# The second layer's experts: engine loops instead of straight code, all shared blocks first

## The reference

```python
h = modulated(layernorm(x))                      # (4096, 128)
logits = h @ gate_w.T + gate_b                   # 8 experts
w, idx = softmax over the top 2 of the logits
def expert(h, w1, b1, w3, b3, w2, b2):           # w1, w3: (256, 128), w2: (128, 128)
    u = (h @ w1.T + b1) * (h @ w3.T + b3)        # (.., 256)
    g, l = min(u[..., ::2], 7), clip(u[..., 1::2], -7, 7)
    return (g * sigmoid(1.702 * g) * (l + 1)) @ w2.T + b2
y = sum over the two chosen e of w_e * expert_e(h)  +  shared_expert(h)
out = x + gate * y
```

## Time and profile before

| | us |
|---|---|
| median of 3 runs | 1839.58 (1836.76 to 1840.22) |
| profiled execution, its own time | 1833.77 |
| its span | 1832.0 |
| granted TensorE clock, mean | 0.877 |
| the mixture's blocks, from the first scatter | 1511 to 1832 |

### The profile page before, as it was taken

One profiled execution on the slowest core, in us unless ns is written; L12 is line 12 of the kernel. 1 busy time (PEld: TensorE's weight loads), 2 busy tenths in 40 slices (PEclk: granted clock), 3 DMA queues, 4 the chain that ended last, 5 costly groups with the idle time before them and its releaser, 6 DMA issues. The chain is left out here.

```text
span 1832.0 us, 41747 instructions
## 1 busy us (share of the span) xinstructions
PE 1461.2 (80%) x15040; PEld 996.7 (54%) x15040; DVE 1314.7 (72%) x3621; ACT 952.3 (52%) x2202; POOL 592.0 (32%) x584
## 2 busy tenths in 40 slices
PE   4277767776698569999999999999999577198490
PEld 2277667776643235555555555555555455187370
DVE  6899999997678736667666676666766685077286
ACT  7555555554311436666666666666666432066260
POOL 0876666770113334111111111111110107601415
PEclk7688888888699789999999999999999867599695
DMA  2400000000000012111111111111110001258352
GB/s 70 132 1 1 1 1 1 1 1 0 12 1 5 15 22 42 31 29 30 29 30 26 25 30 28 30 30 30 30 28 8 15 1 54 71 154 231 95 140 82
DMA packets 150357, 71.53 MB, mean 39 GB/s; under 512 B 95234, under 2 KB 135700, under 8 KB 150164
## 3 DMA queue, kind: packets, MB, share of 16 engines
q1 hardware_dynamic: 143316, 60.42, 15.1%
q0 software_dynamic: 4096, 8.40, 1.5%
q10 hardware_dynamic: 2752, 0.26, 0.1%
HBM read 38.11 MB, written 18.35 MB: 31 GB/s over the span
## 5 line engine op out<-in xcount | busy, mean ns | idle before, releaser
L1299 DVE TENSOR_REDUCE ntop<-score 128x1 f32<-128x512 f32 x512 | 317.9, 683 | 252.0 <-PE score L1178 252.0
L1256 ACT ACTIVATE prob<-score,ntop 128x512 f32<-128x512 f32 x512 | 317.5, 688 | 268.6 <-DVE ntop L1299 268.6
L440 ACT ACTIVATE hist<-zp 128x168 f32<-128x168 f32 (+1 forms) x768 | 224.4, 313 | 171.1 <-DVE zp L408 170.4
L1214 PE MATMUL turned<-ident,prob 128*128 128x128 f32 x2048 | 268.5, 280 | 1.8 <-DVE probT L1240 1.8
L490 PEld LDWEIGHTS py<-hist,diagC 128*128 128x128 f32 x2048 | 262.6, 214 | 0.0
L490 PE MATMUL py<-hist,diagC 128*128 128x128 f32 x2048 | 262.3, 296 | 0.0
L1178 PE MATMUL score<-ks,qs 64*128 64x512 f32 x1024 | 255.0, 616 | 0.0
L1214 PEld LDWEIGHTS turned<-ident,prob 128*128 128x128 f32 x2048 | 219.0, 141 | 49.1 <-issue 28.1
L460 POOL TENSOR_TENSOR xb<-xc,Bm 128x1024 f32<-128x1024 f32 x128 | 244.9, 1954 | 1.3
L403 DVE TENSOR_TENSOR gp<-hist,Ap 128x168 f32<-128x168 f32 (+1 forms) x768 | 229.7, 328 | 14.8 <-POOL xb L460 14.8
L408 DVE TENSOR_TENSOR zp<-gp,xb 128x168 f32<-128x168 f32 (+1 forms) x768 | 232.9, 333 | 0.0
(11 more groups left out here) (304 smaller groups left out, 1624.9 us busy)
## 6 DMA issues: line engine op xcount, KB each, us to landing
w<-in_ew SPq DMA_DIRECT2D x46, 320.0 KB
tb<-in_table SPq DMA_DIRECT2D x64, 127.1 KB
sorted_h<-nought SPq DMA_DIRECT2D x2, 2944.0 KB, 17.2
xs<-sorted_h SPq DMA_DIRECT2D x46, 128.0 KB
sorted_y<-ysb SPq DMA_DIRECT2D x46, 128.0 KB
ks<-k_sb SPq DMA_DIRECT2D x32, 128.0 KB
rel_q<-q_sb SPq DMA_DIRECT2D x248, 8.0 KB
key_q<-q_sb SPq DMA_DIRECT2D x248, 8.0 KB
```

The source lines that it names most:

```text
L440: nc.scalar.activation(hist[:, par, u, lo:hi], zp[j][:, 0:hi - lo], ACT.Tanh)\
L1214: last = nc.tensor.transpose(turned_ps[BANK[e]][:, j * P:(j + 1) * P], prob[G % 2][e][:, j * P:(j + 1) * P], ident[:, :])
L1256: nc.scalar.activation(prob[G % 2][e][:, :], score_ps[r][:, :], ACT.Exp, bias=ntop[:, G % 2, e:e + 1]).then_inc(prob_ready, 1)
L1299: v.tensor_reduce(ntop[:, G % 2, e:e + 1], score_ps[r][:, :], AX.X, ALU.max, negate=True)\
```

## The change

The ORDER becomes 16 shared, then 46 routed (SHARED_FIRST = 16). The rest follows from it or comes beside it:

- ScalarE, VectorE and TensorE go through most blocks in loops that the engines run themselves (Fori). ScalarE: blocks 0 to 3 written out, 5 laps of 2, blocks 14 to 21 written out, 9 laps of 4, the rest written out. VectorE: blocks 0 to 3 written out, 6 laps of 2, then 23 laps of 2. TensorE: 18 steps written out, 5 laps of 8, 6 steps written out.
- No combine is left inside the block sequence; all 32 tiles are combined at the end.
- The routed blocks' biases are picked by TensorE (four small products of the bias rows with a mask, before block 2) and one ScalarE copy; VectorE only makes the mask.
- Weight buffers 5 becomes 8, `xs` buffers 4 becomes 8, gather semaphores 4 becomes 2. SyncE loads 8 blocks' weights first, then 8 blocks of rows, and stores each block at once, not five late. The 8 weight buffers share two semaphores, four to each.
- The places are counted in quarters of 8 tiles (three doubling steps instead of four, the rest by TensorE), and one semaphore of the attention's output weights is merged into another.

```diff
-    NW, NX, NY, NGOT = 5, 4, 4, 4
+    NW, WG, NX, NY, NGOT = 8, 4, 8, 4, 2
+    LAP = 8
     N = NSHARED + NROUTED
-    AFTER = NW
-    SHARED_FIRST, SELECT_AT, IN_LOOP, EVERY = 11, 4, 8, 2
+    SHARED_FIRST = 16
+    SLOTS_AHEAD = NX
+    SELECT_AT = 2
...
-            load_slots(0)
+            for m in range(NW):
+                load_weights(m)
+            for m in range(SLOTS_AHEAD):
+                load_slots(m)
             for m in range(NROUTED):
-                if m + 1 < NROUTED:
-                    load_slots(m + 1)
-                load_weights(m)
-                if m >= AFTER:
-                    store(m - AFTER)
-            for m in range(NROUTED - AFTER, NROUTED):
+                if m + NW < NROUTED:
+                    load_weights(m + NW)
                 store(m)
+                if m + SLOTS_AHEAD < NROUTED:
+                    load_slots(m + SLOTS_AHEAD)
...
-            def select_biases():
-
-                mine = done[:, :, :, :].rearrange("p s n e -> p (s n) e")
-                chain(v.tensor_tensor(mine, eidf[:, :, :].rearrange("p s n -> p (s n)").unsqueeze(2)
...
-                for c in range(4):
-                    chain.add(v.tensor_tensor(bprod[:, :, c, :], mine,
...
-                v.tensor_reduce(bsel[:, :, :], bprod[:, :, :, :], AX.X, ALU.add).then_inc(eid_ready, 1)
-                dve.wait_ge(eid_ready, 2)
...
-            for n in range(N + 1):
-                if n == SELECT_AT:
-                    select_biases()
-                if n < N:
-                    gates(n)
+            def stretch(n0, turns, tile=None):
+
+                with dve.Fori(0, turns) as i:
+                    for u in range(2):
+                        q = (n0 + u) % 2
+                        bias = routed_bias(2 * i + (n0 - SHARED_FIRST + u))
+                        gates(2 * i + (n0 + u), q, bias)
+                        join(2 * i + (n0 - 1 + u), 1 - q)
+                        lins(2 * i + (n0 + u), q, bias)
...
+            for n in range(0, 4):
+                gates(n, n % 2, shared_bias)
                 if n >= 1:
-                    join(n - 1)
-                if n < N:
-                    lins(n)
-                k = combine_at.get(n)
-                if k is not None:
-                    dve.wait_ge(y_taken, shared_at[k // HALVES] + 1)
-                    combine(k)
+                    join(n - 1, (n - 1) % 2)
+                lins(n, n % 2, shared_bias)
+            with dve.Fori(0, 6) as i:
...
+            dve.wait_ge(sel_ready, 1)
+            stretch(SHARED_FIRST, NROUTED // 2)
+            join(N - 1, (N - 1) % 2)
+            dve.wait_ge(y_taken, N)
             for k in range(NT):
-                if k not in combine_at.values():
-                    dve.wait_ge(y_taken, shared_at[k // HALVES] + 1)
-                    combine(k)
+                combine(k, k % NGOT, k // NGOT + 1)
                 if k % TPB == TPB - 1:
                     finish(k // TPB)
...
+            def select():
+
+                pe.wait_ge(eid_ready, 2)
+                for c in range(4):
+                    last = mm(XT[0][:, c * NROUTED:(c + 1) * NROUTED],
+                              b1_rows[:, :].rearrange("e (p c) -> e c p", c=4)[:, c, :], mine[:, :],
+                              start=True, stop=True)
+                last.then_inc(spots_ps, 1)
+
+            for n in range(0, 18):
+                if n == SELECT_AT:
+                    select()
+                if n + 1 == SHARED_FIRST:
+                    pe.wait_ge(sel_ready, 1)
+                block_step(n)
+            with pe.Fori(0, 5) as i:
+                for u in range(LAP):
+                    q = u % 2
+                    turn(LAP * i + (3 + u), (3 + u) % NX, 1 - q, i + ((3 + u) // NX + 1))
+                    up_routed(LAP * i + (18 + u), LAP * i + (2 + u), (2 + u) % NW, q, WG * i + WG * ((2 + u) // NW + 1))
+                    down(LAP * i + (16 + u), q, W[u])
+            for n in range(58, N + 2):
+                block_step(n)
```

More of the change, by code:

```diff
@@ L34 @@
 ALPHA = 1.702
-PARTS = 2
-PT = NT // PARTS
 SLOTS = 2 * P
@@ L41 @@
 NSHARED = NB * SEQ // SLOTS
-RB = 2 * PT * P // SLOTS + NE1 - 1
-NROUTED = PARTS * RB
-MOST = PT * P // SLOTS
+QT = 8
+QUARTERS = NT // QT
+PART_QUARTERS = (2, 2)
+PARTS = len(PART_QUARTERS)
+PT = [QT * q for q in PART_QUARTERS]
+T0 = [sum(PT[:s]) for s in range(PARTS + 1)]
+RB = [2 * t * P // SLOTS + NE1 - 1 for t in PT]
+R0 = [sum(RB[:s]) for s in range(PARTS + 1)]
+NROUTED = R0[PARTS]
+MOST = max(PT) * P // SLOTS
+PART_OF = [s for s in range(PARTS) for _ in range(RB[s])]
 class Chain:
@@ L1562, in _ @@
             for s in range(PARTS):
-                for k in range(s * PT, (s + 1) * PT):
+                for k in range(T0[s], T0[s + 1]):
                     for r in range(2):
@@ L1568, in _ @@
                 for i in range(NY):
-                    pool.wait_ge(y_out[i], 16 * stores(i, (s + 1) * RB))
-                for k in range(s * PT, (s + 1) * PT):
+                    pool.wait_ge(y_out[i], 16 * stores(i, R0[s + 1]))
+                for k in range(T0[s], T0[s + 1]):
                     if k >= NGOT:
@@ L1624, in _ @@
-            for n in range(N + 2):
-                if n + 1 < N and ORDER[n + 1][0] == "routed":
-                    slots(ORDER[n + 1][1])
-                if n < N:
-                    if n == SHARED_FIRST:
-                        act.wait_ge(eid_ready, 2)
-                    gate(n)
-                if 1 <= n <= N:
-                    tanh(n - 1)
-                if n < N:
-                    lin(n)
-                if n >= 2:
-                    take(n - 2)
+                if not (isinstance(n, int) and n < 2):
+                    act.wait_ge(gg_raw, n - 1)
@@ new lines, in take, with take_shared, take_routed @@
+            def take(n, q, dst):
+                act.wait_ge(y_ready, n + 1)
+                A.copy(dst, Y[q][:, 0:SLOTS]).then_inc(y_taken, 1)
+            def take_shared(n, q, i):
+                dst = acc[:, i * HALVES:(i + 1) * HALVES, :] if isinstance(i, int) else acc[:, bass.ds(i * HALVES, HALVES), :]
+                take(n, q, dst.rearrange("p o e -> p (o e)"))
+            def take_routed(n, q, slot, laps):
+                if not (isinstance(laps, int) and laps == 0):
+                    act.wait_ge(y_out[slot], 16 * laps)
+                take(n, q, ysb[slot][:, :, :].rearrange("p o e -> p (o e)"))
@@ new lines, in block_step @@
+            def block_step(n):
+                if n + 1 < N and ORDER[n + 1][0] == "routed":
+                    slots(ORDER[n + 1][1], ORDER[n + 1][1] % 2)
+                if n < N:
+                    gate(n, n % 2, bias_of(n))
+                if 1 <= n <= N:
+                    tanh(n - 1, (n - 1) % 2)
+                if n < N:
+                    lin(n, n % 2, bias_of(n))
+                if n >= 2:
+                    kind, i = ORDER[n - 2]
+                    if kind == "shared":
+                        take_shared(n - 2, n % 2, i)
+                    else:
+                        take_routed(n - 2, n % 2, i % NY, i // NY)
@@ new lines, in _ @@
+            for n in range(14, 22):
+                if n == SHARED_FIRST:
+                    act.wait_ge(sel_ready, 1)
+                block_step(n)
+            with act.Fori(0, 9) as i:
+                for u in range(NY):
+                    q = u % 2
+                    n, m = NY * i + (22 + u), NY * i + (NY + 2 + u)
+                    slots(NY * i + (NY + 3 + u), 1 - q)
+                    gate(n, q, routed_bias(m))
+                    tanh(NY * i + (22 - 1 + u), 1 - q)
+                    lin(n, q, routed_bias(m))
+                    take_routed(NY * i + (22 - 2 + u), q, u, i + 1)
@@ L1650, in _ @@
                                   expn[:, :].unsqueeze(2).to_broadcast([P, NE1, NE1]), ALU.is_lt))
-            for i in range(2):
-                chain.add(v.memset(upto[i][:, :, 0, :], 0.0))
             dve.wait_ge(logits_ready, NBLK)
@@ L1868, in down @@
-                last.then_inc(y_ready, 1)
-            for n in range(N + 2):
-                if n + 1 < N and ORDER[n + 1][0] == "routed":
-                    turn(ORDER[n + 1][1])
-                if n < N:
-                    up(n)
-                if n >= 2:
-                    down(n - 2)
+                    if seeded:
+                        k = shared_block * HALVES + o
+                        mm(Y[q][:, cols], cwT[:, k * P:(k + 1) * P], b2[:, :], start=True, stop=False)
+                    last = mm(Y[q][:, cols], a[:, q, cols], w[:, 4 * P:5 * P], start=not seeded, stop=True)
@@ new lines, in down, with block_step @@
+                last.then_inc(y_ready, 1)
+            def block_step(n):
+                if n + 1 < N and ORDER[n + 1][0] == "routed":
+                    m = ORDER[n + 1][1]
+                    turn(m, m % NX, m % 2, ring(m, NX))
+                if n < N:
+                    kind, m = ORDER[n]
+                    if kind == "shared":
```

(9 more changed lines are left out.)

283 lines of the change are left out of this document (148 added, 135 removed).

## The result

The changed kernel takes 1854.32 us (median of 4, 1853.55 to 1855.49) against 1838.51 us of the kernel before, which ran again beside it: a ratio of 1.0087, 95% interval 1.0069 to 1.0104, so 15.8 us more. The forecast was 1848. The profiled execution took 1854.10, with a span of 1852.3 us and a mean granted clock of 0.873 against 1832.0 and 0.877. Layer one and the attention are as before: the first scatter leaves at 1509.01, before at 1511.36.

The account below looks back on a forecast made before the run. The prediction took two holes of about 45 and 30 us beside GpSimd's indirect DMAs as the bound. Its terms, 17.0 - 3 - 3 - 3.4 - 1.5 - 4 + 6 = +8.1, gave 1848 us, own range 1834 to 1866.

Parts of the forecast that it names:

- The likeliest case: Whole kernel: both holes stay, the change costs +8.1 us, 1848 as the median, range 1834 to 1866; chance 0.52.
- Step 1: Ahead of the routed blocks: five shared blocks of 3.39 us move onto the path, first hole's end unchanged, +17.0 us.
- Step 2: Early shared blocks: bias selection, 5.3 us on VectorE, leaves that engine, -3 us.
- Steps 3 to 5: Routed stretch: last routed block not behind shared products, -3; no additions inside, -3.4; weights and rows eight blocks ahead, -1.5.
- step 7: Block sequence: the engines' loops add bookkeeping, 0.27 us over the slack in each of VectorE's 23 laps, +6 us.
- step 3: End of the routed blocks: the last one no longer waits behind shared products on TensorE, -3 us.
- Step 6: Tail: VectorE is free for additions when the second gather starts, some 11 us sooner, -4 us.
- rival D: Gathers: with two semaphores GpSimd waits for the tile two back, +11 us at the end, 1859; chance 0.05.
- Rival C: Routed stretch: VectorE's laps cost more, 1.6 us each, and pace it, +36 us, 1876; chance 0.13.
- Rival B: Both holes: they come from the supply of straight code, so loops end them, 1752 us; chance 0.30.
- five blocks: First hole: five blocks pass with one instruction packet landed, so an engine starved four times for code would have received it.
- GpSimd's doing: Holes beside scatters and first gather, about 45 and 30 us: they depend on GpSimd, not on the number of blocks.

Follow-up runs that it names:

- the changed kernel with two paces: Changed kernel with the second half's scatters and first gather each held back until ScalarE takes given blocks: 1746.18 us, 0.9982 of the kernel before.
- the three suspects undone: Changed kernel with loops written out, VectorE picking biases, and SyncE waiting for the scatter before asking for weights: 1749.40 us, 1.0008 of the kernel before.

## Why the forecast held, and where it was off

The whole forecast was right in its place (the holes stay, the five shared blocks pay) and in its sign; the sizes were off in both directions. The likeliest case's own range, 1834 to 1866, holds the 1854.3, but the sum of +8.1 is half of the measured +15.8 (and of the +20.3 of the two traces less than half).

*Step 1, +17.0.* The mechanism held, and the step alone measures what it should: 1626.83 in place of 1626.5. That the two agree so closely is partly luck: with 16 first one block fewer had passed at the hole's end, but the hole ended 2.4 us earlier (1600.28 against 1602.67). In the changed kernel it is +31.7, and this is the mis-sized term. The forecast had "the first hole ends when it does now", which is so (90.9 us after the first scatter, before 91.3), but it took for granted that as many blocks pass before that. The block that starts at its end was block 10 before, block 9 with only the order changed, and block 6 in the changed kernel. Four blocks at 3.4 are 13.6 us. Against the kernel with only the order changed, the changed one's first routed block stands 14.0 us later after the first scatter (129.86 against 115.86 us); the whole spans differ by 8.2. I had counted the hole by its end and not asked what its opening depends on. Undoing the loops, SyncE's early loads or TensorE's selection won back none, one and one block, each in one trace. What is left (buffers, shared semaphores, stores at once, counts) and whether the parts add up stays open.

*Step 2, -3.* The path to the scatter got 2.35 us shorter, but the selection itself gained nothing that could be told: with VectorE choosing again the first routed block came sooner, not later.

*Steps 3 to 5, together -7.9.* They fall in the same two stretches as step 7's +6, so the forecast for these is -1.9. Measured are -1.8 up to the first gather and -1.4 between the gathers, together -3.3; no run separates the steps. The last routed block's up start to the second gather is 9.1 us in place of 10.6, half of step 3.

*Step 6, -4.* It is -5.7, and -5.4 in the kernel with only the order changed, so it comes from the order and not from the additions' place. The forecast had read that VectorE's additions wait for each other at 1.06 us as long as GpSimd works. In the changed kernel they don't: eight take 3.05 us in the middle of the second gather (the line at 1812.90). No second-gather delay by two semaphores: GpSimd's 32 gathers take 40.3 us against 40.6, and rival D is out.

*Step 7, +6.* The pair of blocks is 0.20 us longer than 2 x 2.42, near the 0.27 assumed (2.65 + 2.39 against 4.84), but the stretch from the first routed block to the first gather is no longer for it, 71.6 us against 73.5. Of those 1.9 us the straight code loses 1.1 at its first routed block (4.73 us to the next, with loops 3.61) and at most 1.2 to late weights (TensorE's products wait for them three times between 1612 and 1683). Where no hole disturbs, on the third chip, 30 blocks in loops took 77.9 us (2.60 each, the changed kernel with two paces) and 28 written out 71.9 (2.57, the three suspects undone): some 1 us over all 46. Rival C is out.

*Rival B* fell, and with it code supply as the cause. ScalarE and VectorE have the first hole with loops and without. In the changed kernel's second hole, at block 46, all three engines are in loops, TensorE is busy 7.7 of 37 us, and from 1712 to 1755 no instruction packet landed at all; these are the only queues that moved anything:

```profile
q0 software_dynamic: 1024, 2.10, 20.7%
q1 hardware_dynamic: 2828, 2.39, 17.9%
```

The forecast's argument from "five blocks" that pass in the hole was misread: two start in it (1543.57 and 1582.09). But the forecast's sentence on what the holes are, "GpSimd's doing", was only half the matter. GpSimd's indirect DMAs are needed, since the hole starts, ends and moves with them and shrinks when they are thinned out by a fifth to a quarter. They are not sufficient: on a third chip the same instructions at the same rate open none, and slow SyncE by nothing. What differs there, no row shows.

## What to carry to other kernels

When a hole in a profile can't be put down to any engine, ask for its opening as well as its end, and count how much work passes through; a step that is moved ahead of it is priced by both. Before tuning around such a hole, run the kernel on several chips: it may be worth 5% on one and not exist on another. If long runs of indirect DMAs are beside work that signals often, let a cheap wait pace them by that work: it took 3.3% off where the hole was, and a similar pacing cost 0.2% where it wasn't.

## What the runs showed of the hardware that I had not expected

- On the chips with holes, after some 10 to 30 us of unbroken scatters at 1.28 us each, ScalarE starts on TensorE's results late, in the changed kernel's first hole by 13 to 54 us (the down product that ended at 1543.94 was taken at 1598.06), while VectorE starts 0.04 us after ScalarE's result.
- There SyncE needs 13.6 to 16.5 us beside the scatters for eight weight issues that take 8.1 us without them.
- Spacing them at 1.53 to 1.63 us on average, in pairs, each pair behind a block taken, is enough: TensorE was busy 45 of 51 and 46 of 52 us.
- The same program took 1748 us on one chip and 1832 to 1839 on two others, all of the difference in this one stage so far as the traces tell: in all of them the first scatter leaves between 1509 and 1513 unless it is held back.
